# Relation passes of a graph network: one chunk of eight comes from TensorE instead of a gather

## The reference, cut to what matters

```python
def _rgat_conv(x, src, dst, etype, W, Q, K, b):
    xw = jnp.einsum('ni,rio->rno', x, W)            # a row of 64 per node and type
    qn = jnp.einsum('rno,roh->rnh', xw, Q)
    kn = jnp.einsum('rno,roh->rnh', xw, K)
    alpha = jax.nn.leaky_relu(qn[etype, dst] + kn[etype, src], NEG_SLOPE)
    amax = jax.ops.segment_max(alpha, dst, num_segments=n)
    ex = jnp.exp(alpha - amax[dst])
    denom = jax.ops.segment_sum(ex, dst, num_segments=n)
    attn = ex / (denom[dst] + 1e-16)
    out_j = xw[etype, src].reshape(-1, H, hc // H)
    agg = jax.ops.segment_sum(attn[:, :, None] * out_j, dst, num_segments=n)
    return agg.reshape(n, hc) + b
```

## Time and profile before

| what | value |
|---|---|
| three runs | 10400.70, 10401.42, 10406.88 us; median 10401.42 us |
| profiled execution | 10397.95 us |
| its span, first to last instruction | 10396.1 us |
| busy in the span | PE 59%, DVE 65%, ACT 20%, POOL 53% |
| mean granted TensorE clock | 0.726 of 2.4 GHz |
| first relation pass | 7562.74 us (first gather issued) to 8609.07 us (last score) |

### The profile page before, as it was taken

How to read it: one execution, slowest core, us unless ns; L and a number is a source line. 1 busy time by engine, 2 the same in 40 slices (tenths; PEclk the granted TensorE clock), 3 DMA queues, 4 the chain that set the end, 5 groups by cost and what they waited for, 6 DMA issues and landing times. The chain is left out here.

```text
span 10396.1 us, 147400 instructions
## 1 busy us (share of the span) xinstructions
PE 6100.9 (59%) x34135; PEld 4519.6 (43%) x34136; DVE 6789.3 (65%) x9297; ACT 2070.2 (20%) x7672; POOL 5531.5 (53%) x5847
## 2 busy tenths in 40 slices
PE   2998998788888766663765666467411116511117
PEld 1776776666666433332753333257300005300007
DVE  7777444677667578888987888899422227422238
ACT  0332555000000112222651222156100000000000
POOL 2776777677677277770004777300067770177750
PEclk9998999899899678885556888655555557655559
DMA  2444555455555288882985888479233334233334
GB/s 61 113 113 102 144 145 139 127 145 148 122 148 146 70 270 292 292 292 86 386 314 174 292 292 292 142 300 386 86 87 81 82 81 97 75 81 81 81 68 115
DMA packets 835417, 1702.28 MB, mean 164 GB/s; under 512 B 386819, under 2 KB 455972, under 8 KB 781431
## 3 DMA queue, kind: packets, MB, share of 16 engines
q1 hardware_dynamic: 442976, 1115.60, 31.1%
q0 software_dynamic: 214112, 420.66, 18.0%
q10 hardware_dynamic: 178256, 165.14, 4.9%
HBM read 1257.06 MB, written 445.40 MB: 164 GB/s over the span
## 5 line engine op out<-in xcount | busy, mean ns | idle before, releaser
L553 POOL DMA_INDIRECT gathered_rows<-node_table,index x2496 | 2374.2, 951 | 1041.9 <-issue 748.7
L553 POOL DMA_INDIRECT gathered_rows<-rel_table,index x1664 | 1569.9, 943 | 1895.7 <-ACT index L543 1389.2
L553 POOL DMA_INDIRECT gathered_rows<-xl_table,index x1664 | 1572.8, 945 | 1554.4 <-issue 1382.1
L573 PE MATMUL ps_sum<-messages,onehots 128*125 128x65 f32 (+3 forms) x13312 | 1982.3, 315 | 551.0 <-DVE messages L1748 248.6
L573 PEld LDWEIGHTS ps_sum<-messages,onehots 128*125 128x125 f32 x13312 | 1885.1, 228 | 683.0 <-issue 677.0
L709 PE MATMUL ps_G<-table_parts,low_onehots 125*128 125x320 bf16 x12480 | 1917.1, 315 | 74.0 <-issue 51.0
L1485 PE MATMUL ps_Z<-xr,onehots_wide 125*128 x3328 | 1378.9, 572 | 760.1 <-DVE z L1533 693.0
L709 PEld LDWEIGHTS ps_G<-table_parts,low_onehots 125*128 125x128 bf16 x12480 | 1270.6, 104 | 626.9 <-issue 63.6
L1485 PEld LDWEIGHTS ps_Z<-xr,onehots_wide 125*128 125x128 f32 x3328 | 763.2, 242 | 1376.3 <-issue 1251.8
L1621 PE MATMUL ps_Q<-query_parts,onehots_turned 125*128 x1664 | 239.8, 259 | 1890.4 <-DMA onehots_turned<-onehots_turned 1890.4
L1621 PEld LDWEIGHTS ps_Q<-query_parts,onehots_turned 125*128 125x128 bf16 x1664 | 173.0, 104 | 1957.2 <-issue 1922.6
(11 more groups left out here) (314 smaller groups left out, 6525.4 us busy)
## 6 DMA issues: line engine op xcount, KB each, us to landing
stash_a<-gathered_rows SPq DMA_DIRECT2D x208, 1300.0 KB
kept_rows<-stash_a SPq DMA_DIRECT2D x208, 1300.0 KB
onehots<-onehots_kept SPq DMA_DIRECT2D x520, 500.0 KB
onehots_turned<-onehots_turned SPq DMA_DIRECT2D x416, 250.0 KB
stash_r<-gathered_rows ACTq DMA_DIRECT2D x208, 272.0 KB
kept_rows<-stash_r SPq DMA_DIRECT2D x208, 272.0 KB
low_rows<-low_rows SPq DMA_DIRECT2D x416, 125.0 KB
onehots_kept<-onehots ACTq DMA_DIRECT2D x104, 500.0 KB
```

Of the source, the lines that this page charges most:

```text
L553: pool.indirect_dma_start(G[:, HALF * k + q, 0:width], None, table, bass.IndirectOffsetOnAxis(IDX[:, k, q:q + 1], 0)).then_inc(gathered[k] ...
L573: return nc.tensor.matmul(ps_sum[0:BN, bass.ds(at, width)], S[:, j, :], M, start=False, stop=True, skip_group_check=True)
```

## The change

In both relation passes GpSimd gathers seven chunks of a group. The eighth chunk's rows are made on chip. TensorE fetches its 128 node rows from the split table (15 matmuls), VectorE picks one of five into `XF` [128 edges, 64], TensorE turns that (`ps_X`), ScalarE copies it to on-chip memory (`XT`), TensorE multiplies it by the weights and keys of all eight types (`ps_W`, 512 + 32 columns, read from `w3` and `wkq` with the type innermost), and VectorE keeps the edge's type (multiply, L1747) and sums over the eight (L1752) into the eighth place of `G`. The stages of one group are spread over four iterations of the loop: one-hots for n+4, fetch for n+3, turn for n+2, multiply and pick for n+1. `ps_Q` shrinks to one place instead of four, since the new tiles need the room. The low source numbers come by 104 more small DMAs a pass on SyncE's queue, and the record `fifth_all` (which fifth of the table a source is in) is stored with the types at the start and read back with them, 448 KB more each way.

```diff
-        types_dram = nc.dram_tensor("types", [P, 2, NS], I32, kind="Internal").ap()
+        types_dram = nc.dram_tensor("types", [P, 3, NS], I32, kind="Internal").ap()
...
+                    sp.dma_start(types_dram[:, 0:2, :], kept).then_inc(s_slotD, 16)
+                    sp.dma_start(types_dram[:, 2, :], fifth_all[:, :].bitcast(I32)).then_inc(s_slotD, 16)
...
-                ps_Q = pb("ps_Q", [P, K, 2, BANK], F32, es)
+                ps_Q = pb("ps_Q", [P, 2, BANK], F32, es)
...
+                by_type = w3[:, l, :, :].rearrange("i r f -> i f r")
+                keys_by_type = wkq[:, l, 0, :, :].rearrange("i r h -> i h r")
...
                             for k in range(K):
                                 chunks_free(sp, i, k)
                                 load_turned(sp, ST, i, k)
+                                if not last_turn:
+                                    load_low_row(sp, LR, i + 1, k, ONE)
...
-                        gather_loop(pool, G, FR, rel_table, IDX, rows_free)
+                        gather_loop(pool, G, FR, rel_table, IDX, rows_free, LAST_J)
...
+                        def turn_rows(i, k):
...
+                            nc.tensor.transpose(ps_X[0:D, 0:P], XF[:, k % 2, :], ident[:, :]).then_inc(rows_turned.sem, 1)
+
+                        def rows_by_type(i, k):
...
+                            pe.wait_ge(rows_kept.sem, rows_kept.at(n + 1))
+                            pe.wait_ge(typed_picked.sem, typed_picked.at(n))
+                            nc.tensor.matmul(ps_W[:, 0:D * R], XT[:, k % 2, :], by_type, start=True, stop=True)
+                            nc.tensor.matmul(ps_W[:, D * R:FR * R], XT[:, k % 2, :], keys_by_type, start=True, stop=True).then_inc(typed_made.sem, 1)
...
                                 pe.wait_ge(loaded[k].sem, loaded[k].at(16 * i + 16))
+                                pe.wait_ge(mult_made.sem, mult_made.at(n))
                                 for q in range(HALF):
...
+                                if not (last_turn and k + 1 >= K):
+                                    rows_by_type(i, k + 1)
+                                if not (last_turn and k + 2 >= K):
+                                    turn_rows(i, k + 2)
+                                if not (last_turn and k + 3 >= K):
+                                    fetch_rows(pe, OT, HP, ps_G, i, k + 3, ONE)
...
+                            nc.scalar.activation(XT[:, k % 2, :], ps_X[0:D, 0:P], ACT.Copy).then_inc(rows_kept.sem, 1)
...
+                            v.tensor_tensor(WB[:, :, :], ps_W[:, 0:FR * R].rearrange("p (f r) -> p f r", r=R),
+                                            T1[:, k, LAST_J, 0:R].unsqueeze(1).to_broadcast([P, FR, R]), ALU.mult).then_inc(typed_picked.sem, 1)
...
+                            v.tensor_reduce(G[:, HALF * k + LAST_J, :], WB[:, :, :], AX, ALU.add).then_inc(row_typed.sem, 1)
...
+                                if not (last_turn and k + 1 >= K):
+                                    types_at(i, k + 1)
+                                    pick_type(i, k + 1)
+                                if not last_turn:
+                                    make_low_onehots(dve, LR, OT, HI, ids, i, k + 4, ONE, fifths)
+                                if not (last_turn and k + 3 >= K):
+                                    pick_row(i, k + 3)
                                 dve.wait_ge(leaky_made.sem, leaky_made.at(n + 1))
                                 dve.wait_ge(dest_made.sem, dest_made.at(n + 1))
...
+                        make_ids(ids)
+                        split_table(HP, rest[:, :, :, :])
```

More of the change, by code:

```diff
@@ L704, in fetch_rows @@
             pe.wait_ge(low_made.sem, low_made.at(n + 1))
-            for g in range(FETCH):
-                pe.wait_ge(bank_picked.sem, bank_picked.at(FETCH * n + g - 1))
+            for g in range(fetch):
+                pe.wait_ge(bank_picked.sem, bank_picked.at(fetch * n + g - 1))
                 for a in range(FIVE):
                     for part in range(3):
-                        last = nc.tensor.matmul(ps_G[:, (FETCH * k + g) % 2, 0:D * FIVE], OT[0:BN, k, g, a, :],
+                        last = nc.tensor.matmul(ps_G[:, (fetch * k + g) % 2, 0:D * FIVE], OT[0:BN, k, g, a, :],
                                                 HP[:, part, a, :, :].rearrange("p f b -> p (f b)"),
@@ L745, in picks_over @@
             for c in (bank_made, bank_picked, row_picked):
-                c.over(FETCH * GROUPS)
+                c.over(fetch * GROUPS)
             table_split.over(1)
@@ L1578, in pair_scores, with relation_scores @@
                     c.over(NCH // QD)
-        def relation_scores(SCORE, XQ, src_type, types):
+        def relation_scores(SCORE, XQ, src_type, types, fifths, l):
             phase[0] += 1
             FR = D + HR
+            ONE = 1
+            LAST_J = HALF - ONE
             es = ExitStack()
@@ L1598, in _, with turn @@
                     def _(sp):
-                        with sp.Fori(0, TURNS) as i:
+                        def turn(i, last_turn):
                             for k in range(K):
@@ L1602, in _ @@
                                 load_turned(sp, ST, i, k)
+                                if not last_turn:
+                                    load_low_row(sp, LR, i + 1, k, ONE)
+                        for k in range(K):
+                            load_low_row(sp, LR, 0, k, ONE)
+                        with sp.Fori(0, TURNS - 1) as i:
+                            turn(i, False)
+                        turn(TURNS - 1, True)
                         for c in stashed:
@@ new lines, in turn @@
+                        def turn(i, last_turn):
+                            for k in range(K):
+                                if not (last_turn and k + 2 >= K):
+                                    keep_turned(i, k + 2)
+                                act.wait_ge(row_typed.sem, row_typed.at(K * i + k + 1))
+                                act.wait_ge(gathered[k].sem, gathered[k].at(16 * LAST_J * (i + 1)))
+                                act.sem_inc(act_seen, 1)
+                                act.dma_start(stash_r[bass.ds(K * i + k, 1), :, :].rearrange("o p r -> (o p) r"),
+                                              G[:, group_of(k), :].rearrange("p c f -> p (c f)")).then_inc(stashed[k].sem, 16)
+                                keep_index(act, IDX, src_type, i + 1, k)
@@ L1634, in _ @@
+                        with act.Fori(0, TURNS - 1) as i:
+                            turn(i, False)
+                        turn(TURNS - 1, True)
                     @block.vector
```

150 lines of the change are left out of this document (112 added, 38 removed).

## The result

The changed kernel took 10309.98 us, the median of four runs (10309.12 to 10311.1), beside 10402.31 us for the kernel before (10400.7 to 10406.88) on the same chip. The ratio is 0.9911, interval [0.9893, 0.9928]: faster by 0.9%, 92 us, where 257 were forecast. The profiled execution took 10311.1 us, with a span of 10309.3.

The account below looks back on a forecast made before the run. GpSimd's gather issue was taken as the bound, before and after. From 10397.95 us, 259.6 for removed gathers came off and 2.5 for set-up was added: 10140.9 profiled, 10144 as median; range 10130 to 10265.

Parts of the forecast that it names:

- the choice of the clock inside a round: TensorE's part per group: other work 3.97 us even at 1.2 GHz, fetch 2.04 at 2.4; part 6.0, round 8.3 us.
- GpSimd's step: Relation-pass gathers: one issue every 1.248 us, also with seven a group, so a group lasts 8.74 us.
- VectorE's prices: Added VectorE work per group, priced by size: 3.39 us on top of 3.02, 6.8 with handovers, hidden under 8.74.
- The loop of waits: TensorE and VectorE wait for each other each group: round is TensorE's part + 2.25 us; part must stay under 6.5.
- The part at the half clock: TensorE's queries, type product, turn and fetch in a group, all at 1.2 GHz: 7.98 us, round 10.2.
- The stride of the weights: Type product reading weights 64 numbers apart: none to 1.56 times longer, 1.2 to 1.9 us at full clock, hidden.
- The rival of the longer round: Relation-pass loop: clock rises only mid-fetch (3.0 us), part 7.0, round 9.2, total about 10267 us; chance 0.11.
- The slow rival: Relation-pass loop stays at the half clock: round 10.2 us, 39 us more a pass, about 10481; chance 0.09.
- No gain: Relation passes: gathers in truth land no faster, leaving the time near 10404 us; chance 0.04.
- The widened range: Whole kernel: own range 10132 to 10160 us, widened upward to 10130 to 10265 to hold 8 in 10.
- The start: Set-up before the first relation pass: recording the fifths adds 0 to 4 us, taken as 2.5.

Follow-up runs that it names:

- four_parts: Changed kernel with twenty matmuls per fetched chunk instead of fifteen, the smallest table part added twice; 10442.0 us, ratio 1.0044 to the kernel before, quick chip.
- two_parts: Changed kernel with ten matmuls per fetched chunk instead of fifteen, the smallest table part left out; 10148.25 us, ratio 0.9762 to the kernel before, quick chip.
- pick_after_copied: Changed kernel with VectorE's pick moved behind product and sum, and weights copied into TensorE's reading order; 10148.32 us, ratio 0.9761 to the kernel before, quick chip.
- filler_8_2: Changed kernel with eight unread matmuls behind each fetch and part numbers moved from PSUM to SBUF, second run; 12337.15 us, ratio 1.0170, slow chip.
- after_2: Not defined by name; apparently the changed kernel, unaltered, run again on a slow chip: 12359.93 us, ratio 1.0193 to the kernel before.

## Why the prediction was wrong

**The step that failed** is the choice of the clock inside a round: "Even if that work is all at 1.2 GHz and the fetch at 2.4, the part is 3.97 + 2.04 = 6.0 and the round 8.3". The fetch took 3.93 us in the mean, so the part is 7.5 us and the round 9.56. In the sum of a round, 3.97 of other work, 2.04 of fetch and 2.25 of pick, product and handovers, the runs put 3.56 + 3.93 + 2.06. The fetch is the term that was mis-sized, and it turned the choice of the bound. A round of 9.56 is 0.82 us over GpSimd's 8.74, which times some 204 groups makes 167 us; 165 are missing. I had taken the rise within one fetch of 60 matmuls as proof that a fetch of 15 would run at 2.4 GHz, though the pick of the first 15 of that very fetch came after 4.01 us. The rise came there at 219.3, as the first 15 ended; here it comes near the end of the 15 or, in three rounds of five, not within them. The 3.97 us of other TensorE work ahead of the fetch, on which I built, did not bring it forward. Why the clock stands as it does in a round is open: four_parts shows no more than that a longer part puts the rise at a fixed place.

**What stood.**
- GpSimd's step: 1.25 us with seven a group. With the loop shortened (two_parts) or cut (pick_after_copied), the time is 10148 us, ratio 0.9762 and 0.9761. Scaled to the first chip's 10401 us that is 10153, 9 us above the forecast. So the arithmetic of the gathers was right, but it describes a kernel in which VectorE's work stands in another order.
- VectorE's prices: type product 0.72 us forecast and measured, its sum 0.72 and 0.72, low one-hots 0.81 and 0.81. Its work in a group is 6.3 us, which pick_after_copied shows in its first groups, when the gathered rows are ahead.
- The loop of waits, with its 2.25 us of handover and pick: 2.06 us. It was named with its limit (part under 6.5), and it is the bound.
- The part at the half clock, 7.98 us: 7.7 in the rounds whose fetch is all at the half clock (7982.11 to 7989.79), since neighbouring matmuls overlap. Its fetch is 4.21 and not 4.01, so such a round is 9.7 to 9.9 us and not 10.2.
- The stride of the weights: no cost at 1.2 GHz. At 2.4 the product with its keys takes 2.13 us (7587.98 to 7590.11), above the 1.2 to 1.9 that were allowed; with the loop closed, the copy is worth 26 us.

**The rival of the longer round** (9.2 us, 10267 us, chance 0.11) described what happened, a little too short. Its mechanism, a clock that rises only in the middle of the fetch, is the right one in kind; it rises still later, and not in every fetch. The evidence for it was in the groups of rows that I cited, and its chance was too low. The slow rival needed a part above 7.6 us, and 7.49 is close to that: four_parts, with 0.68 us more, is slower than the kernel before by 0.4%. "No gain" is out. The widened range would have taken in 10265 us; the measured 10310 is beyond it.

**The start.** The first pass begins 6.8 us later than before, where 0 to 4 were allowed for the set-up. The other kernels with the same set-up begin it 0.5 to 10.5 us later (four_parts at 7563.24, pick_after_copied at 7573.28), so this term is not known better than that. The first gathers of a pass take 2.18, 2.95 and 2.58 us instead of 0.94, 4.9 us more in all, which I had not counted. The two engines' rows:
```profile
7569.37 1.52 DVE L684 CAST table_parts<-H 125x1600 bf16<-125x1600 f32 x1
7570.92 2.90 DVE L685 TENSOR_TENSOR table_rest<-H,table_parts 125x1600 f32<-125x1600 f32 x1
...
7569.53 2.18 POOL L555 DMA_INDIRECT gathered_rows<-rel_table,index  x1 [955.87 <-ACT index L545]
7572.01 2.95 POOL L555 DMA_INDIRECT gathered_rows<-rel_table,index  x1 [0.30 <-issue]
7575.26 2.58 POOL L555 DMA_INDIRECT gathered_rows<-rel_table,index  x1 [0.30 <-issue]
7578.15 0.94 POOL L555 DMA_INDIRECT gathered_rows<-rel_table,index  x1 [0.30 <-issue]
```
They are long just while VectorE splits the table, SBUF to SBUF, until 7577.7. The trace of before had it too, at its own split: 206.29, 208.32 and 211.59 with 1.72, 2.97 and 2.58 us. The Trainium skill ("SBUF — State Buffer", section on SBUF's two separate sides) tells of a copy of f32 numbers by VectorE from SBUF to SBUF, in its two-port mode, which locks GpSimd out of the port pair through which it writes a DMA's descriptors. The trace agrees in that the gathers are long beside such work; it doesn't show the port. And the second gather starts at 7572.01, in the middle of a subtraction (until 7573.82), and should have ended at 7572.95, before the next cast begins; so it isn't casts alone that hold a gather up. In the changed kernel this is hidden by the longer rounds. In a kernel that is bound by GpSimd it costs its 4.9 us a pass, most of the 9 us above.

## What to carry to other kernels

When a change makes two engines wait for each other within one iteration, write down the loop: its period is the sum of the parts around it, and it has to fit under the engine that is the bound now, at either clock level of TensorE. Then look whether one of the two could release the other first; moving VectorE's pick behind its product and sum was worth 1.25% on a quick chip, on top of the copied weights, more than the change itself. And a mean clock says nothing until it is set beside what TensorE does in the same microsecond.

## What the runs showed of the hardware

- The granted clock of a periodic load can stand against the work: with 7.5 us of work and 2.06 of pause in a round it is 0.54 in the long matmuls and 0.88 in the pause. It need not be the same in each round: here five rounds of different length repeat, and with five matmuls more (four_parts) all rounds are alike.
- A moving operand with a stride of 64 f32 numbers costs nothing at 1.2 GHz (2.04 us for 512 columns) and 0.9 us at 2.4 (1.98 instead of 1.09).
- GpSimd's indirect DMAs take two to three times their 0.94 us while VectorE splits a table within SBUF. Those that overlap a VectorE comparison take 1.09 us when both its operands are in SBUF (filler_8_2), and 0.95 when one is in PSUM (after_2).
- The kernel before differs by 17% between two kinds of chip, and the changed kernel by 20% (10310 and 12360 us) with GpSimd busy 5346 and 5360 us and VectorE 7462 and 7472. The change differs in sign between them: 0.9911 and 1.0193. Moving the pick makes a kernel that is faster than both kernels on the slow chips (0.9965), and with the copied weights on a quick one (0.9761). It is the one to go on from; with both edits it has not run on a slow chip.
